# A decoder layer on one Trainium2 core: other slots around the cross-attention merge, an opening in a new order, and a last store by batch

## The reference

```python
# 1. self-attention, 16 heads of 64, everything cut to steps of 1/4096 in +-8
qkv = x @ w_qkv.T;  q, k, v = make_fxp(...)
dots = make_fxp(q @ k.T * scale);  attn = make_fxp(softmax(dots))
out = make_fxp(attn @ v);  x = x + make_fxp(out @ w_proj.T + b_proj)
# 2. cross-attention, 16 heads of 64, keys and values from ctx, plain float32
x = x + softmax((ln(x) @ Wq) @ (ctx @ Wk).T * scale) @ (ctx @ Wv) @ Wo + bo
# 3. feed-forward, 2 of 8 low-rank experts on shared weights
for k in 0, 1:  out += top_v[k] * (relu(h @ wi.T + (h @ A_k.T) @ B_k.T) @ wo.T)
```

## Time and profile before

| | |
|---|---|
| time, median of 3 runs (us) | 652.91 (652.76 to 653.82) |
| the profiled execution: its own time / its span (us) | 653.37 / 651.3 |
| PE, DVE, ACT, POOL busy (us) | 637.1, 503.2, 414.2, 359.8 |

### The profile page before, as it was taken

The page is one execution under the profiler, slowest core; times in us unless marked ns, Lnnn a source line. Parts: engine busy times, 40 slices in busy tenths (PEclk is TensorE's granted clock), DMA queues, the critical chain, the costliest instruction groups (busy, mean ns, idle before and its releaser), DMA issues.

```text
span 651.3 us, 16062 instructions
## 1 busy us (share of the span) xinstructions
PE 637.1 (98%) x5339; PEld 549.7 (84%) x5339; DVE 503.2 (77%) x970; ACT 414.2 (64%) x1458; POOL 359.8 (55%) x760
## 2 busy tenths in 40 slices
PE   8899999999999999999999999999999999999997
PEld 4688888888888888887888888888888888988986
DVE  4888789988898889976777677766666758888765
ACT  2788788888888888886554566465555454444432
POOL 4996476765676676864587778555356632010100
PEclk9999999999999999999999999999999999999999
DMA  7954000000000000031100000000000000010010
GB/s 228 389 228 175 1 2 2 2 1 0 0 0 0 0 1 0 16 130 66 47 3 17 2 2 1 18 2 3 1 0 0 0 1 1 2 33 17 15 34 32
DMA packets 10405, 23.93 MB, mean 37 GB/s; under 512 B 1634, under 2 KB 6034, under 8 KB 9458
## 3 DMA queue, kind: packets, MB, share of 16 engines
q1 hardware_dynamic: 8050, 14.90, 6.7%
q0 software_dynamic: 1872, 7.87, 3.4%
q10 hardware_dynamic: 432, 0.52, 0.2%
HBM read 21.19 MB, written 2.10 MB: 36 GB/s over the span
## 4 chain that ended last, share of the span: by engine, by line
PE 74%; ACT 5%; DVE 3%; issue 2%; POOL 1%; ACTq 0%; DVEq 0%; POOLq 0%
PE bank L575 17%; PE bank L577 16%; PE bank L576 16%; PE bank L771 5%; PE bank L747 4%; PE bank L759 4%; PE bank L640 3%; PE bank L663 3%; ACT e_sb L1063 3%; PE bank L629 2%; PE bank L593 1%; PE bank L894 1%; ACT aT_sb L967 1%; DVE neg_max L1325 1%; DVE hid L1419 0%
## 5 line engine op out<-in xcount | busy, mean ns | idle before, releaser
L438 POOL TENSOR_SCALAR p_f<-e_sb,rsum 128x128 f32<-128x128 f32 x256 | 92.2, 386 | 82.4 <-DVE rsum L1368 82.0
L346 POOL TENSOR_SCALAR p_int<-e_sb,rsc 128x128 int16<-128x128 f32 x256 | 106.7, 438 | 6.3 <-issue 5.9
L1063 ACT ACTIVATE e_sb<-bank,neg_max 128x128 f32<-128x128 f32 x256 | 89.9, 386 | 1.6 <-DVE neg_max L1325 1.6
L962 ACT ACTIVATE sgn<-bank 128x512 bf16<-128x512 f32 x96 | 54.5, 606 | 34.3 <-PE bank L577 34.2
L977 ACT ACTIVATE e_sb<-si 128x128 f32<-128x128 int16 x256 | 76.1, 315 | 0.0
L1049 ACT ACTIVATE q_sb<-bank 128x512 f32<-128x512 f32 x32 | 19.2, 599 | 86.9 <-PE bank L577 86.9
L1185 DVE SCALAR_TENSOR_TENSOR ri<-sgn,bank 128x512 int16<-128x512 bf16 x96 | 63.3, 684 | 12.6 <-ACT sgn L962 11.3
L1063 ACT ACTIVATION_READ_ACCUMULATOR e_sb<-bank,neg_max 128x1 f32 x256 | 58.0, 226 | 0.0
L977 ACT ACTIVATION_READ_ACCUMULATOR e_sb<-si 128x1 f32 x256 | 52.9, 206 | 0.0
L575 PE MATMUL bank<-xnT_hi,wqk_lo 128*128 128x512 f32 x128 | 52.8, 413 | 0.0
L577 PE MATMUL bank<-xnT_hi,wqk_hi 128*128 128x512 f32 x128 | 50.2, 392 | 0.0
(11 more groups left out here) (157 smaller groups left out, 2136.1 us busy)
## 6 DMA issues: line engine op xcount, KB each, us to landing
wB_raw<-in_wB SPq DMA_DIRECT2D x1, 3072.0 KB, 14.5
wB_hi<-in_wB POOLq DMA_DIRECT2D x1, 3072.0 KB, 11.5
wqk_raw<-in_wqk SPq DMA_DIRECT2D x8, 256.0 KB, 6.3
out<-x_sb SPq DMA_DIRECT2D x8, 256.0 KB, 2.2
wqk_hi<-in_wqk POOLq DMA_DIRECT2D x7, 256.0 KB, 7.6
x_sb<-in_x SPq DMA_DIRECT2D x3, 512.0 KB, 19.9
wp_raw<-in_wp SPq DMA_DIRECT2D x1, 1024.0 KB, 14.2
wp_hi<-in_wp POOLq DMA_DIRECT2D x1, 1024.0 KB, 8.3
```

Source lines behind the costliest of these rows:

```text
L346: i = nc.gpsimd.tensor_scalar(p_int[:, half, t, :], e_sb[:, half, t, :], rsc[:, half, t:t + 1], -0.5, ALU.mult, ALU.add)
L438: i = nc.gpsimd.tensor_scalar(p_f[:, half, t, :], e_sb[:, half, t, :], rsum[:, half, t:t + 1], 0.0, ALU.mult, ALU.add)
L962: nc.scalar.activation(sgn[:, m % 2, :], proj_ps[m % 2][:, :], ACT.Sign).then_inc(a_sgn, 1)
L1063: last = nc.scalar.activation(e_sb[:, (s - 1) % 2, t, :], s_ps[hh][:, (t % 4) * P:(t % 4 + 1) * P], ACT.Exp, bias=neg_max[:, t:t + 1], sca ...
```

## The change

It has five parts.

1. **Opening.** ACT, not a transfer, rounds the weight parts qk 1, qk 2 and v 1 (`high_part`). PE transposes the first normed batches one by one as DVE delivers them; DVE applies the norm ahead of the `_lo` part of weight 0; `ident_b` is made later; `keep_busy` issues 20 matmuls in place of 26. In slots 0 to 2 of group 0 PE computes the next slot's q block ahead of this slot's scores, and DVE clips q ahead of the integer of k. POOL's `_lo` parts move by about a slot.
2. **`inv_std`.** The factor of `units` goes into `veps`, one POOL instruction less; in the later groups of phase A it stands ahead of `a_weights` in slot 1.
3. **Slots of phase B.** In slot 0 of groups 1 to 3 ACT takes four exponentials ahead of the copy of q, and DVE the maxima ahead of `cT_lo`. In slot 3 `oT_hi` comes ahead of `b_y_out`. In group 0 DVE's `y_out` moves from ahead of the k copy to behind the reciprocal.
4. **Merge.** ACT's copy and the tile `merge` go; DVE adds the bank to `cw_raw` directly, behind the reciprocal and ahead of `oT_lo`. PE waits for that sum ahead of the second half of the next slot's transposes, where it waited for the copy ahead of the first.
5. **End.** The last group collects in four banks (`last_ps`), one batch in each; DVE adds, and SP and ACT store, batch by batch.

```diff
 inv_std:
-                nc.gpsimd.tensor_scalar(veps[:, :], mv[:, :, 1], EPS, None, ALU.add).then_inc(g_veps, 1)
+                unit = (FIX * GROW) ** -2.0 if scaled else 1.0
+                nc.gpsimd.tensor_scalar(veps[:, :], mv[:, :, 1], EPS, unit, ALU.add, ALU.mult).then_inc(g_veps, 1)
                 wait(pool, g_veps, n + 1)
-                i = nc.gpsimd.tensor_tensor(rstd[:, :], veps[:, :], mhalf[:, :], ALU.pow)
-                if scaled:
-                    i.then_inc(g_pow, 1)
-                    wait(pool, g_pow, n + 1)
-                    i = nc.gpsimd.tensor_tensor(rstd[:, :], rstd[:, :],
-                                                units[:, bass.ds(n, 1), :].rearrange("p a b -> p (a b)"), ALU.mult)
-                i.then_inc(g_rstd, 1)
+                nc.gpsimd.tensor_tensor(rstd[:, :], veps[:, :], mhalf[:, :], ALU.pow).then_inc(g_rstd, 1)
...
 POOL a_slot:
+                if not first and s == 1:
+                    inv_std(g + 1, scaled=not last)
                 if not (first and s == 0):
                     a_weights(NP * g + s - 1, (s - 1) % 2)
-                if not first and s == 1:
-                    inv_std(g + 1, scaled=True)
...
-            for part in LOW_ORDER[0:6]:
+            for part in LOW_ORDER[3:6]:
                 load_high(*part)
...
 PE:
-            keep_busy(26)
-            pe.wait_ge(g_const, 6)
+            keep_busy(20)
+            pe.wait_ge(g_const, 4)
...
+                if not (first and 0 < s <= LAG):
+                    block(s, 0)
+                block(s, 1)
...
+                if first and s < LAG:
+                    block(s + 1, 0)
                 a_scores(n, s, BLOCKS * g + 3 * s + 2)
 
-            normed_T(0, lambda: None)
+            for b in range(GB):
+                wait(pe, *((ln_xn, 1) if b == GB - 1 else (ln_x0, b + 1)))
+                for kt in range(KD):
+                    last = pe.transpose(proj_ps[kt][:, b * P:(b + 1) * P], xn[:, b, kt * P:(kt + 1) * P], ident[:, :])
...
 PE b_transpose:
                 for hh in range(2):
+                    if hh == 1 and summed:
+                        pe.wait_ge(m_sum, summed)
...
 PE, last group of phase C:
+                    last_group = drain or (last and s >= 3)
                     for b in range(GB):
-                        last = split3(y_ps[b // 2][:, (b % 2) * D:(b % 2 + 1) * D],
+                        bank, col = (last_ps[b], 0) if last_group else (y_ps[b // 2], (b % 2) * D)
+                        last = split3(bank[:, col:col + D],
...
 ACT:
+            def high_part(j):
+                kind, i = LOW_ORDER[j]
+                act.wait_ge({"qk": ld_qk, "v": ld_v}[kind][i], 16)
+                raw, hi, _ = low_part(kind, i)
+                nc.scalar.copy(hi, raw).then_inc(w1_hi, 1)
+
             xnT_high(0)
+            high_part(0)
+            high_part(1)
...
 ACT b_slot:
+                    if ahead:
+                        exps(0)
                     wait(act, b_S, 2 * n - 2)
                     wait(act, b_blk, BLOCKS * g + 3 * s + 1)
...
-                if s == LAG and not first:
+                if drain and s == LAG:
                     b_y_out(g)
-                if merging and s in (3, 4, 5, 6):
-                    act.wait_ge(m_mm, s - 2)
-                    wait(act, m_sum, s - 3)
-                    nc.scalar.copy(merge[:, :], pT_ps[1][:, :]).then_inc(m_out, 1)
...
                     nc.scalar.copy(oT_hi[:, :], o_ps[:, :]).then_inc(b_ohi, 1)
+                if s == LAG and not first and not drain:
+                    b_y_out(g)
...
 DVE b_slot:
+            def merged_sum(c):
+
+                if c == 0:
+                    dve.wait_ge(ld_wi, 16)
+                dve.wait_ge(m_mm, c + 1)
+                kt, cols = merge_chunk(c)
+                w = cw_raw[:, kt, cols].rearrange("p a f -> p (a f)")
+                V.tensor_tensor(w, w, pT_ps[1][:, :], ALU.add).then_inc(m_sum, 1)
...
+                if first and s == LAG:
+                    y_out(G)
+                if merging and s in (3, 4, 5, 6):
+                    merged_sum(s - 3)
                 if lagged:
                     wait(dve, b_ohi, n - LAG + 1)
...
 end:
+            def add_last_rows(b):
+                wait(dve, c_y, b + 1)
+                xx = x_sb[:, (G - 1) * GB + b, :]
+                V.tensor_tensor(xx, xx, last_ps[b][:, 0:D], ALU.add).then_inc(c_xb, 1)
...
+            for b in range(1, GB, 2):
+                act.wait_ge(c_xb, b + 1)
+                nc.scalar.dma_start(out[(G - 1) * GB + b], x_sb[:, (G - 1) * GB + b, :]).then_inc(out_done, 16)
```

More of the change, by code:

```diff
@@ L160, in build @@
     up_ps = banks[4:8]
+    last_ps = banks[0:4]
     def sem(name):
@@ L672, in a_slot, with block @@
                 lagged = not (first and s < LAG)
+                if first and s == LAG:
+                    pe.wait_ge(idb, 1)
                 if lagged:
                     a_transpose(n - LAG, (s - LAG) % 2)
-                if first and s > 0:
-                    wait(pe, w_lo, low_count("qk", s))
-                for i in range(2):
-                    a_block(g, 3 * s + i, [w[:, s, :, i, :] for w in (wqk_hi, wqk_lo)])
+                def block(t, i):
+                    if first and t > 0 and i == 0:
+                        wait(pe, w_lo, low_count("qk", t))
+                    a_block(g, 3 * t + i, [w[:, t, :, i, :] for w in (wqk_hi, wqk_lo)])
+                if not (first and 0 < s <= LAG):
+                    block(s, 0)
+                block(s, 1)
                 def project(batches=range(GB)):
@@ L1000, in a_slot @@
                 sign_of(g, 3 * s + 2)
+                if first and s == 0:
+                    high_part(2)
                 if lagged:
@@ L1039, in b_slot, with exps @@
                 lagged = not (first and s < LAG) and not (drain and s >= LAG)
+                def exps(hh):
+                    if hh == 0:
+                        if first and s in (1, 2):
+                            wait(act, a_p, NP * G - 2 + s)
+                        wait(act, b_p, n - 2)
+                        wait(act, b_rs, n - 1)
+                    wait(act, b_mx, 2 * n - 1 + hh)
+                    for t in range(GB * hh, GB * hh + GB):
+                        last = nc.scalar.activation(e_sb[:, (s - 1) % 2, t, :], s_ps[hh][:, (t % 4) * P:(t % 4 + 1) * P], ACT.Exp,
+                                                    bias=neg_max[:, t:t + 1], scale=-1.0,
+                                                    accum_out=sums[:, t:t + 1])
+                    if hh == 1:
+                        last.then_inc(b_e, 1)
+                ahead = s == 0 and not first and not drain
                 if not drain:
@@ L1055, in b_slot @@
                 if (not (first and s == 0)) and not (drain and s >= 1):
-                    if first and s in (1, 2):
-                        wait(act, a_p, NP * G - 2 + s)
-                    wait(act, b_p, n - 2)
-                    wait(act, b_rs, n - 1)
-                    for hh in range(2):
-                        wait(act, b_mx, 2 * n - 1 + hh)
-                        for t in range(GB * hh, GB * hh + GB):
-                            last = nc.scalar.activation(e_sb[:, (s - 1) % 2, t, :], s_ps[hh][:, (t % 4) * P:(t % 4 + 1) * P], ACT.Exp,
-                                                        bias=neg_max[:, t:t + 1], scale=-1.0,
-                                                        accum_out=sums[:, t:t + 1])
-                    last.then_inc(b_e, 1)
-                if s == LAG and not first:
+                    if not ahead:
+                        exps(0)
+                    exps(1)
+                if drain and s == LAG:
                     b_y_out(g)
-                if merging and s in (3, 4, 5, 6):
-                    act.wait_ge(m_mm, s - 2)
-                    wait(act, m_sum, s - 3)
-                    nc.scalar.copy(merge[:, :], pT_ps[1][:, :]).then_inc(m_out, 1)
                 if first and s < LAG:
@@ L1160, in norm_apply @@
                                         mv[:, b, 0:1], rstd[:, b:b + 1], ALU.subtract, ALU.mult)
[L1161 removed]
+                    if isinstance(n, int) and n == 0:
+                        i.then_inc(*((ln_xn, 1) if b == GB - 1 else (ln_x0, 1)))
+                if GB - 1 in batches and not (isinstance(n, int) and n == 0):
                     i.then_inc(ln_xn, 1)
@@ L1251, in a_slot @@
                 lagged = not (first and s < LAG)
-                qk(g, s, n)
+                qk(g, s, n, first and s < LAG)
                 if first and s == 2:
@@ L1326, in b_slot @@
                                         ALU.min).then_inc(b_mx, 1)
+                if s == 0 and not first and not drain:
+                    wait(dve, b_chi, g + 1)
+                    V.tensor_tensor(cT_lo[:, :], cT_raw[:, :], cT_hi[:, :].bitcast(F32), ALU.subtract).then_inc(b_clo, 1)
                 if first and 1 <= s <= LAG:
@@ L1355, in b_slot @@
```

(7 more changed lines are left out.)

87 lines of the change are left out of this document (41 added, 46 removed).

## The result

The changed kernel takes 647.96 us (median of 4 runs, 647.88 to 648.28), against 652.97 (652.76 to 653.82) for the kernel before beside it, here as the median of four: ratio 0.9922, 95% interval 0.9905 to 0.9939. The profiled execution spans 645.9 us, 5.4 less than the 651.3 of before, at the full clock.

A forecast was written before the change was run, and what follows sets the result against it. PE's stream of matmuls sets the time, so only fewer PE waits or shorter ends help. Terms +0.5 - 1.4 - 1.6 - 0.6 - 2.0 - 0.6 = -5.7 us give 647.2 us, range 644.8 to 650.2.

The forecast's parts named there:

- Head: Start of the opening: earlier `xn` and transposes by batch start the first q block near 10.6, not 11.37: -0.75 us.
- Slots 0 to 2: Opening's q blocks ahead of scores: waits move through DVE's list; opening as a whole +0.5 us, ends -0.3 and +0.8.
- Its own sign of being wrong: Opening: scores to next v rows not the 4.2 of now, as when POOL's moved subtractions meet DVE.
- the first rival: Opening pays in full: waits ahead of the scores filled without a new one, -3.0 in place of +0.5, 643.7; 13%.
- `inv_std` ahead: Phase A: POOL delivers `rstd` a slot earlier, DVE's wait of 1.97 us in group 1 (5.3 in all) goes: -1.4 us.
- in proportion: Phase A: PE's loss scaled from group 1 to all DVE waits, 0.75 x 5.3 / 1.97 = 2.0 at most.
- Slot 0 of groups 1 to 3: Phase B: four exponentials move into ACT's wait for the q block: 1.8 at most, taken as -1.6 us.
- Slot 3: Phase B: `oT_hi` ahead of two copies gives time back in groups 2 and 3: -0.6 us; group 0: 0.
- Merge: Phase B, group 1, slots 3 to 6: merge adds leave POOL, copies leave ACT: -2.0 us, from -2.2 to -1.0.
- End: End of the kernel: four banks, sums follow batches at PE's pace, last sum and store halved: -0.6, between -0.3 and -0.8.
- the rival of a falling clock: Opening: PE's longer waits drop the clock until slot 3, doubling the loop's PE part: +12 us, 659; 4%.

The follow-up runs named there:

- at home: Changed kernel with the opening's q blocks back in their own slots, each ahead of its own slot's scores: 645.30 us, ratio to before 0.9868.
- after: The changed kernel itself, all five parts of the change against the kernel before: 647.96 us, ratio 0.9922.
- the eviction's order: Changed kernel with ScalarE evicting the output projection ahead of `oT_hi` again in slot 3 of each phase B group: 648.92 us.
- the kernel with the late `cw_lo`: Version with q blocks in their own slots (645.30), POOL's last `cw_lo` quarter moved to the end of phase B: 654.02 us.

## Why the prediction was right, and where not

The forecast was 647.2 with its mechanism as the likeliest; measured are 647.96. By the profiled span the sum was -5.7 and the change -5.4; the runs' medians differ by 5.0. That the sum is so near is in part luck, as the items show.

*Head.* Right: -1.07 in this profile (10.30 against 11.37) for -0.75; the ten other profiles of the same head have -0.46 to -1.04. `xn` starts 0.70 earlier here, for 0.4; transposes by batch would be the rest, which no run separates.

*Slots 0 to 2.* Right to a few tenths at every place: scores 16.46, 23.64, 31.05 for 16.7, 23.8, 31.05, v rows 20.62, 28.07, 35.57 for 20.85, 28.1, 35.5, and +0.54 in all for +0.5. Two misses cancel in it: counted from the first q block to the scores of slot 3, the slots cost 27.92 - 26.31 = 1.6 us for 1.25, and the head gave 0.3 more. Its argument, that the time from scores to v rows goes through DVE's list and doesn't shrink, is borne out by both orders (4.16 to 4.52 us with the blocks ahead, 4.36 to 5.01 at home, 4.17 to 4.78 before). What the prediction did not see is that this part held edits of opposite worth. The blocks ahead lose 2.7 us; the clips' order gains 2.0 with the blocks at home, of which 1.1 pay for what the rest of part 1, POOL's moved parts by all that the rows show, costs the slots. It priced only their sum, by old distances. Its own sign of being wrong, POOL's moved subtractions meeting DVE, came about in one place (the k clip of slot 2 takes 0.95 us in after, 0.42 before). Of the first rival's -3.0, 1.9 could be had, by the opposite order: at home the opening ends at 35.78 against 37.68.

*`inv_std` ahead.* Phase A gave -1.55 for -1.4, but not by the step named. Neither the order nor the multiplication, nor both together, bring it back (0.25 us at most): what is left is the 0.6 us by which POOL's three instructions are quicker with `veps` in its new form, and whose cause stays open. The step that failed is "in proportion": the wait of DVE costs PE next to nothing up to about 1.4 us, and from there each 0.2 us costs 0.2 in slot 3 (1.55, 1.76, 1.97 us of wait: 0.15, 0.38, 0.58). Each edit that shortens it further, as the order does, finds nothing left to gain. The -1.4 came near because most of the cost lies in the last 0.6 us of the wait, which no run brings back.

*Slot 0 of groups 1 to 3.* Over-sized: -0.9 (-0.54, +0.06 and -0.44) for -1.6. Group 2 has nothing, because `cT_lo`, which the change moved behind the maxima, falls beside POOL's `cw_lo`. That DVE instruction was in the diff and the prediction gave it no line. *Slot 3*: -0.68 in groups 2 and 3 for -0.6; putting it back costs 1.0 by the medians, with 0.16 in group 1 too. Group 0 gave -0.16, for 0.

*Merge.* Right in sum: group 1 falls by 2.68, of which 0.54 is slot 0's, so -2.1 for -2.0. Undoing the merge alone gives back 1.6 and the eviction's order 0.16 in this group; the rest is of no edit by itself. The `xn` pair takes 1.23 us for "under 1.6". No row of PE waits for the sum on DVE.

*End.* -0.54 for -0.6; no run undoes it. *The clock* stayed full in the opening, with three waits of 1.4 to 1.7 us: the rival of a falling clock, which made the change slower, did not come. That the clock can fall within the work is shown by the kernel with the late `cw_lo`, but behind a wait of 7 us and not of 1.5.

The best version measured is the changed kernel with the q blocks at home, 645.30 us.

## What to carry to other kernels

Before work is put into a wait, ask whether the wait is one or the first of two in a loop: here the q block filled the gap ahead of the scores and left the gap behind them, in which it had cost nothing. A change of several edits that comes out near zero is worth taking apart, since it may be a gain and a loss. And undo an edit before it is given the credit, and undo the whole of it: here a wait of a side engine cost next to nothing up to about 1.4 us, and what took it below that can be another edit than the one meant for it.

## What the runs showed of the hardware

*DVE beside POOL.* `cT_lo` (two inputs in the on-chip memory) took 1.19 us beside POOL's `cw_lo` and 0.68 without it. When `cT_lo` started first, it kept its 0.69 and `cw_lo` took 1.86 in place of 1.42. The Trainium skill, "SBUF — State Buffer", section "Who interferes with whom", has a lock of a port pair that the two engines share, held for a whole instruction by the one that issues first, and a DVE instruction with two inputs in that memory contends for it; the rows of `cT_lo` agree with it. Clips of `ri`, with one such input, took 1.01 and 0.94 us beside POOL's low parts, 0.42 with POOL idle, and 0.42 beside `p_int` too. Which of POOL's instructions stretch them, and why, the runs don't separate.

*The clock after a long wait.* A wait of PE of 7.0 us was followed by 3.5 us at 0.50 (the lower of the two levels, 1.2 GHz) and 6 us at a mean of 0.83, with full load, and cost 2.8 us on top of itself. Waits of 1.4 to 1.7 us, three times 7 us apart, left the granted clock full.
